# Another order for the fills of one PSUM bank in an audio-tower kernel

## The reference, cut to what matters

```
h = tok(x)                                   # convolution, ReLU, batch normalisation
h = h + attn(layernorm(h))                   # 8 heads, softmax over 746 keys
h = h + gate * expert[argmax(layernorm(h) @ Wr + br)](layernorm(h))
```

## Time and profile before

| | |
|---|---|
| median of 3 runs | 1467.63 us (1467.03 to 1468.56) |
| profiled execution, its own time | 1461.96 us |
| its span in the trace | 1460.1 us |
| PE busy | 1339.3 us (92%) |
| DVE busy | 1083.7 us (74%) |
| ACT busy | 978.0 us (67%) |
| POOL busy | 589.2 us (40%) |
| chain that ended last, by engine | PE 79%, DVE 11%, ACT 3%, DMA 2%, POOL 2% |

### The profile page before, as it was taken

How to read it: one execution, slowest core, us unless ns; L and a number is a source line. 1 busy time by engine, 2 the same in 40 slices (tenths; PEclk the granted TensorE clock), 3 DMA queues, 4 the chain that set the end, 5 groups by cost and what they waited for, 6 DMA issues and landing times.

```text
span 1460.1 us, 31108 instructions
## 1 busy us (share of the span) xinstructions
PE 1339.3 (92%) x9928; PEld 757.9 (52%) x9928; DVE 1083.7 (74%) x3005; ACT 978.0 (67%) x2735; POOL 589.2 (40%) x538
## 2 busy tenths in 40 slices
PE   6738899999999999999999999999999985799996
PEld 3423344454545454454545454544444432799996
DVE  4329878788887888888888878888888613477775
ACT  1321487777878787878777787878776782477774
POOL 0004223353535343444435363434442122456665
PEclk9999799999999999999999999999999996799998
DMA  3041522415040514223150505142232041333331
GB/s 52 1 87 28 76 65 33 91 28 111 23 102 31 88 50 68 68 51 82 37 110 8 117 17 101 45 74 65 54 79 40 16 138 39 104 105 105 105 105 53
DMA packets 70139, 96.78 MB, mean 66 GB/s; under 512 B 14637, under 2 KB 60029, under 8 KB 70016
## 3 DMA queue, kind: packets, MB, share of 16 engines
q1 hardware_dynamic: 61232, 75.73, 25.0%
q0 software_dynamic: 7872, 18.54, 4.4%
q10 hardware_dynamic: 912, 0.94, 0.3%
HBM read 56.72 MB, written 39.00 MB: 66 GB/s over the span
## 4 chain that ended last, share of the span: by engine, by line
PE 79%; DVE 11%; ACT 3%; DMA 2%; POOL 2%; issue 2%; SPq 1%; POOLq 0%; DVEq 0%; ACTq 0%
PE psum L1076 18%; PE psum L1094 17%; PE psum L1108 14%; DVE half_max L869 7%; PE psum L1140 6%; PE psum L1150 6%; PE psum L983 3%; PE psum L1042 3%; PE psum L1012 3%; PE psum L995 2%; PE psum L1020 2%; PE psum L1036 2%; PE psum L1048 1%; ACT p_ring L635 1%; DVE stats L734 1%
## 5 line engine op out<-in xcount | busy, mean ns | idle before, releaser
L869 DVE TENSOR_REDUCE half_max<-psum 128x1 f32<-128x373 f32 x1536 | 771.3, 537 | 186.5 <-PE psum L1108 184.7
L635 ACT ACTIVATE p_ring<-psum 128x373 f32<-128x373 f32 (+1 forms) x1536 | 688.0, 494 | 273.6 <-PE psum L1094 190.9
L1108 PE MATMUL psum<-k_rows,q_rows 96*128 96x373 bf16 x1536 | 506.0, 332 | 26.5 <-DMA k_rows<-k_parts_dram 20.7
L1094 PE MATMUL psum<-q_rows,k_rows 98*128 98x373 bf16 (+1 forms) x1536 | 496.7, 328 | 3.7 <-ACT p_ring L635 2.9
L1076 PE MATMUL psum<-p_ring,values 128*32 128x373 f32 (+1 forms) x3072 | 321.1, 490 | 2.4 <-ACT o_un L648 2.1
L1094 PEld LDWEIGHTS psum<-q_rows,k_rows 98*128 98x128 bf16 (+1 forms) x1536 | 156.6, 103 | 297.1 <-ACT p_ring L635 192.3
L525 POOL DMA_INDIRECT routed_rows_dram<-rows,pos_i x96 | 96.0, 1000 | 363.8 <-DVE tok_id L863 178.8
L1108 PEld LDWEIGHTS psum<-k_rows,q_rows 96*128 96x128 bf16 x1536 | 154.1, 100 | 115.9 <-DVE half_max L869 44.4
L565 POOL DMA_INDIRECT out_dram<-p_ring,slot_id x102 | 121.1, 1187 | 84.2 <-DVE p_ring L962 67.0
L1076 PEld LDWEIGHTS psum<-p_ring,values 128*32 128x32 f32 (+1 forms) x3072 | 61.1, 108 | 104.9 <-issue 61.8
L549 POOL TENSOR_TENSOR rstd<-var_eps,minus_half 128x6 f32<-128x6 f32 x16 | 21.6, 1347 | 162.5 <-DVE var_eps L746 162.5
(11 more groups left out here) (156 smaller groups left out, 1600.8 us busy)
## 6 DMA issues: line engine op xcount, KB each, us to landing
q_rows<-q_parts_dram SPq DMA_DIRECT2D x192, 93.2 KB, 3.2
k_rows<-k_parts_dram SPq DMA_DIRECT2D x192, 93.2 KB, 4.5
p_ring<-routed_rows_dram SPq DMA_DIRECT2D x102, 130.0 KB
q_parts_dram<-q_part SPq DMA_DIRECT2D x16, 559.5 KB, 3.0
k_parts_dram<-k_part SPq DMA_DIRECT2D x16, 559.5 KB, 3.0
seq<-in_w_dram SPq DMA_DIRECT2D x1, 2048.0 KB, 8.7
seq<-in_w_dram SPq DMA_DIRECT2D x8, 256.0 KB, 6.5
out_dram<-p_ring,slot_id POOLq DMA_INDIRECT x102
```

What stands on the lines that cost most here:

```text
L635: last = nc.scalar.activation(probs[0:kn(kt), G % N_P, j, :], st_of(i, s)[0:kn(kt), 0:HALF], ACT.Exp)
L869: nc.vector.tensor_reduce(half_max[:, s:s + 1], mx_bank[s % N_MX][:, 0:HALF], AX.X, ALU.max)\
L1094: last = nc.tensor.matmul(st_of(i, s)[0:kn(kt), 0:HALF], k_rows[par][0:KM, h, D * kt:D * kt + kn(kt)], q_rows[par][0:KM, h, qh * HALF:(qh ...
L1108: nc.tensor.matmul(mx_bank[s % N_MX][:, 0:HALF], q_rows[1 - par][0:KR, h, D * t:D * (t + 1)], k_rows[1 - par][0:KR, h, half * HALF:(half + ...
```

## The change

It moves entries in the two lists, and with them the steps in which ACT and DVE evacuate:

- The first half of `V` goes from step 22 to step 6, ahead of all others. The four fills of `OT0` and `OT1` go from 6, 10, 14, 18 to 10, 14, 18, 22. `PROJ` 0 stays at 26; `V` 1 goes from 34 to 30, and `PROJ` 1 from 30 to 34.
- `MT` goes from (16, 17, 18, 24, 25, 26) to (17, 18, 19, 25, 26, 27). The multiplications that it waits for go from steps 12 and 20 to steps 16 and 24.
- `Q`, `K`, `MAX0`, `LOGIT` and `RANK` move one step later, with their evacuations. `XN2T` goes from (50, 51, 53, 54, 56, 57) to (54, 55, 57, 58, 59, 61), and the statistics before it from steps 33 to 38 to steps 37 to 42.

```
-        FILLS = (("OT0", 0, 6), ("OT0", 1, 10), ("OT1", 0, 14), ("OT1", 1, 18), ("V", 0, 22), ("PROJ", 0, 26),
-                 ("PROJ", 1, 30), ("V", 1, 34), ("MAX1", 0, 38), ("Q", 0, 45), ("Q", 1, 49), ("K", 0, 53), ("K", 1, 57),
-                 ("MAX0", 0, 61), ("LOGIT", 0, 65), ("RANK", 0, 77))
-        BESIDES = {"HTOK": (0, 1, 2, 3, 5, 6), "MT": (16, 17, 18, 24, 25, 26), "XNT": (36, 37, 38, 40, 41, 42),
-                   "XN2T": (50, 51, 53, 54, 56, 57)}
+        FILLS = (("V", 0, 6), ("OT0", 0, 10), ("OT0", 1, 14), ("OT1", 0, 18), ("OT1", 1, 22), ("PROJ", 0, 26),
+                 ("V", 1, 30), ("PROJ", 1, 34), ("MAX1", 0, 38), ("Q", 0, 46), ("Q", 1, 50), ("K", 0, 54), ("K", 1, 58),
+                 ("MAX0", 0, 62), ("LOGIT", 0, 66), ("RANK", 0, 78))
+        BESIDES = {"HTOK": (0, 1, 2, 3, 5, 6), "MT": (17, 18, 19, 25, 26, 27), "XNT": (36, 37, 38, 40, 41, 42),
+                   "XN2T": (54, 55, 57, 58, 59, 61)}
...
-                    if s in (46, 47, 50, 51) and live(i, 2):
-                        q_or_k(i, "Q", (s - 46) // 4, (s - 46) % 4)
+                    if s in (47, 48, 51, 52) and live(i, 2):
+                        q_or_k(i, "Q", (s - 47) // 4, (s - 47) % 4)
...
-                    if s in (7, 8, 11, 12, 15, 16, 19, 20) and live(i, -1):
-                        normalise(i, i - 1, (s - 7) // 8, (s - 7) % 8 // 4, (s - 7) % 4)
+                    if s in (11, 12, 15, 16, 19, 20, 23, 24) and live(i, -1):
+                        normalise(i, i - 1, (s - 11) // 8, (s - 11) % 8 // 4, (s - 11) % 4)
...
-                    if s in (23, 35) and live(i, 1):
-                        bias_values(i, par, s // 35)
+                    if s in (7, 31) and live(i, 1):
+                        bias_values(i, par, s // 31)
...
-                    if s in (27, 31) and live(i, -1):
-                        residual(i, i - 1, s // 31)
-                    if 33 <= s < 39 and live(i, -1):
-                        if s == 33:
+                    if s in (27, 35) and live(i, -1):
+                        residual(i, i - 1, s // 35)
+                    if 37 <= s < 43 and live(i, -1):
+                        if s == 37:
```

More of the change, by code:

```diff
@@ L652, in body @@
                         max_out(i, i, 1, "MAX1")
-                    if s in (46, 47, 50, 51) and live(i, 2):
-                        q_or_k(i, "Q", (s - 46) // 4, (s - 46) % 4)
-                    if s in (54, 55, 58, 59) and live(i, 2):
-                        q_or_k(i, "K", (s - 54) // 4, (s - 54) % 4)
-                    if s == 62 and live(i, 1):
+                    if s in (47, 48, 51, 52) and live(i, 2):
+                        q_or_k(i, "Q", (s - 47) // 4, (s - 47) % 4)
+                    if s in (55, 56, 59, 60) and live(i, 2):
+                        q_or_k(i, "K", (s - 55) // 4, (s - 55) % 4)
+                    if s == 63 and live(i, 1):
                         max_out(i, i + 1, 0, "MAX0")
-                    if s == 75 and live(i, -1):
+                    if s == 76 and live(i, -1):
                         act.wait_ge(s_rt, (i - 1) * 10 + 7)
@@ L884, in body @@
                         norm_rows(nc.vector, lambda t: xn[:, t, :], lambda t: h_cur[:, t, :], mv, rstd, s_ln_p)
-                    if s in (27, 31) and live(i, -1):
-                        residual(i, i - 1, s // 31)
-                    if 33 <= s < 39 and live(i, -1):
-                        if s == 33:
+                    if s in (27, 35) and live(i, -1):
+                        residual(i, i - 1, s // 35)
+                    if 37 <= s < 43 and live(i, -1):
+                        if s == 37:
                             dve.wait_ge(s_free, fill(i, "PROJ", 1))
-                        layer_stats(i - 1, s - 33, rows, stats2, mv2, var_eps2, s_ln2)
+                        layer_stats(i - 1, s - 37, rows, stats2, mv2, var_eps2, s_ln2)
                     if s == 46 and is_body(i, LAST_BODY):
@@ L897, in body @@
                         split(dve, nc.vector, s_apart_v, i, "K")
[L898 to L903, removed]
+                    if 67 <= s < 75 and live(i, -1):
+                        router(i, i - 1, s - 67)
+                    if 78 <= s < 80 and live(i, -1):
+                        router(i, i - 1, s - 70)
+                    if 80 <= s < 86 and live(i, -1):
+                        ranks(i, i - 1, s - 80)
             run_bodies(dve, body)
```

## The result

The changed kernel takes 1483.04 us (1481.5 to 1484.9, 4 runs) against 1467.33 (1466.98 to 1468.56, 4 runs). The ratio is 1.0106, with a 95% interval of 1.0089 to 1.0124: 15.7 us slower, where 16.2 were forecast (1483.8 against 1467.6 at that time).

The account below looks back on a forecast made before the run. PE was taken to set the pace, each of its waits being time. Halves of +0.64 and +0.6 made 1.24 in each of 13 bodies, with the other bodies +16.2 us: 1483.8, 8 in 10 within 1471 to 1491.

Parts of the forecast that it names:

- The first half: Steps 6 to 27 of a body: PE waits of 2.92 instead of 2.17, less 0.11, so +0.64 us per body.
- The chain of 1.23: From a maximum through DVE's reduction and multiplication to PE's start: 1.23 us, which any distance from a maximum obeys.
- 0.16 for its backlog: Step 17: added to DVE's lateness of 0.22 at most, since a fill behind a wait runs longer; wait 1.06.
- The second half: Waits before Q 1, K 0, K 1 and MAX0 for ACT's evacuations: 0.83 instead of 0.25, about +0.6 per body.
- The covers: Hidden work: POOL's norms ready 0.4 ahead of XN2T; nearly 7 us remain for SP's last load to land.
- what it is late by: Price if POOL's cover for XN2T fails; rival with POOL late by 0.5 in 13 bodies: 1490, chance 0.07.
- The sum: Whole kernel: 13 bodies at 1.24 give 16.1; with bodies 0, 14, 15 and 16, +16.2 us.
- the rest: Outside bodies 1 to 13: body 0 +1.0, body 14 about 0, body 15 -1.2, body 16 +0.3.
- what follows: After body 14: body 15 loses its wait for ACT's copy, -1.2; body 16 has a fill behind transposes, +0.3.
- The clock rival: Clock falls behind each of 28 new PE waits, 50 us more: 1534, chance 0.02.
- The drop at 1162: Granted clock fell to 0.56 there; body 15's copy wait and the slow clock behind it were to go: -1.2.
- The rule of the Trainium skill: Frequent small idle stretches between matmul groups can swing the clock; it spoke against the change but was given little weight.

Follow-up runs that it names:

- with DVE relieved: Changed kernel with output fills one step earlier (9, 13, 17, 21) and statistics at steps 5, 6, 8, 12, 13, 16: ratio 0.9824 to the kernel before.
- The last experiment: Changed kernel with XN2T back at steps 50 to 57 while its statistics stay at 37 to 42: ratio 1.0537 to the kernel before.
- the first four experiments: MT three steps later (0.9999), second half undone (1.0055), output fills one step earlier (0.9919), all on the changed kernel; second half alone on the kernel before (1.0049).
- the last four: Earlier fills with early statistics (0.9824), that with second half undone and MT later (0.976), MT nearer on the kernel before (1.0107), XN2T back on the changed kernel (1.0537).

## Why the prediction was right

**The first half.** Forecast and measured waits at steps 6, 10, 14, 17, 22 and 25: 0, 0, 0.55, 1.06, 0.41, 0.90 against 0, 0, 0.59, 0.94, 0.41, 0.90. The chain of 1.23 from a maximum to whoever waits for the multiplication held to 0.01 where DVE was not behind. Where it was, at 17, I had added 0.16 for its backlog; it came to 0.04. From the end of multiplication 12 (639.97 to 640.23 in the changed kernel) to reduction 16 (642.52) DVE took 2.29, where I had counted 2.42, and PE's side took 2.24 instead of 2.20. That it is the place of `MT` and not V's is shown by moving `MT` in each kernel: away from the multiplication in the changed one (-1.12 per body), towards it in the one before (+1.16).

That the chain is late because `weigh` stands ahead of the maximum is shown most cleanly by the fill of 22: one step earlier, with no statistics near it and no fewer steps behind its multiplication, it lost its 0.41. Elsewhere `MT`'s distance and DVE's backlog moved along. One step earlier, the fills no longer waited, except where DVE was full; with DVE relieved the waits there fell to 0.02 before the fill of 13 and 0.17 before the transpose at 17.

**The second half.** Forecast 0.38, 0, 0.18, 0.27, measured 0.40, 0, 0.17, 0.19. The last was off because I took 0.17 as the free distance from a maximum to `MAX0`'s transposes; it is 0.25. The same 0.09 stood in my figure for the kernel before, where `MAX0` does not wait, so it fell out of the difference: about 0.6 was forecast, and alone the half costs 0.55 per body.

**The covers.** POOL's norms end at 670.41 and their first transpose starts at 670.95, so, with 0.14 for the hand-over as in the earlier trace rows, the 0.4 of cover were there. The last experiment gave the price when it is gone: 2.8 per body for the wait, as forecast ("what it is late by"), and on average 1.7 more through the clock, which the term for this case left out.

**The sum.** 1.13 in each full body against 1.24. From the start of the span to the tables behind the pipeline (L1124 at 1239.32 and 1254.94) the change costs 15.6 us against 16.2, in one profiled execution of each; the medians differ by 15.7. It is closer than its parts, and that is luck: bodies 1 to 13 cost 14.6 instead of 16.1, and the rest 1.0 instead of 0.1 (body 0 1.2 instead of 1.0, body 14 0.3 instead of 0, what follows -0.5 instead of -0.9). The profiled spans differ by more, 20.4, since the expert stage behind the tables took 225.6 instead of 220.8 with the same instructions. The change is not the cause. On the chip of the first four experiments this stage took 219.7 to 221.5 in all four traces, on that of the last four 224.5 to 226.6, whatever the kernel, so the two profiled executions were most likely made on different chips. (That of the kernel before, 1461.96, also lies 5 us below all its other runs.)

**The clock rival** did not come true: 1.00 over the whole body after, with its waits of up to 0.94. The drop at 1162 of the kernel before is gone too, as forecast: the granted clock is 1.00 from 1160 to 1228 in the trace after. A falling clock is a real mechanism of this kernel all the same, at a wait of 2.8. The rule of the Trainium skill that I weighed (TensorE: Matmul & The Clock Gate, section "A second HAM failure mode: psum-queue depth-cycling": frequent small idle stretches can make the clock swing) does not describe this kernel: many short waits per body left the clock alone, and one long one lowered it in nine of twelve bodies.

## What to carry to other kernels

In engines that run in lockstep, price an evacuation by where its trigger stands and not by a count of steps. A consumer one step behind it waits for the whole chain (here 1.23 us, of which 0.33 would pass anyway), and a batch of long matmuls put between the two takes its place for nothing if the trigger is issued ahead of the batch. An engine that is busy 84% on average can still be the limit over eight steps; spread its side work before moving anything else.

## What the runs showed that I had not expected

- A wait of 2.8 us of PE in a body that is otherwise full lowered the granted clock (0.59 over the 2.7 us behind it in the body shown) in nine of twelve bodies, at 1.3 to 4.4 us more each. Waits up to 1.3 left it at 1.00.
- The same kernel differs by 6 to 7 us between chips (1460.4 against 1466.6 and 1467.3), nearly half of what the change costs, so only ratios on one chip tell such changes apart. Some 5 of them lie in the expert stage.
- Two halves of a change that each cost 0.55 to 0.58 per body can hide one another: with `MT` moved far back the first half turned into a gain of 0.55, and the sum looked like no change.
